# Row-tiled weighing in a two-layer graph network kernel: pairs of 64-row matmuls, bias by its own bf16 matmul, and a new split of the product sums

## The reference

```python
# layer 0: h has 64 values an edge, w has 4 paths of 8 x 8
h = jax.nn.relu(edge_feat @ W1 + b1)
w = (h @ W2 + b2).reshape(e, 4, MUL, MUL)
m0 = ALPHA * (einsum('ei,eio->eo', s_e * sh0, w_000) + C110 * einsum('eim,em,eio->eo', v_e, sh1, w_110))
m1 = ALPHA * (einsum('ei,em,eio->eom', s_e, sh1, w_011) + einsum('eim,eio->eom', v_e * sh0, w_101))
out0 = segment_sum(m0, dst); out1 = segment_sum(m1, dst)
# layer 1: the same with 64 hidden values from one distance an edge, weights R, spherical harmonics Y of the
# edge's direction, and an einsum over paths
R = jax.nn.relu(abs_distances[:, None] @ w1 + b1) @ w2 + b2
x = _layernorm(x + layer(x))   # after each layer
```

## Time and profile before

| | |
|---|---|
| median of 3 runs | 4531.57 us (4531.0 to 4543.85) |
| profiled execution | 4544.37 us, span 4542.6 us |
| mean granted TensorE clock | 0.922 of full speed |
| busy: PE, PEld, DVE, ACT, POOL | 83%, 49%, 87%, 52%, 70% |

### The profile page before, as it was taken

How to read it: one execution, slowest core, us unless ns; L and a number is a source line. 1 busy time by engine, 2 the same in 40 slices (tenths; PEclk the granted TensorE clock), 3 DMA queues, 4 the chain that set the end, 5 groups by cost and what they waited for, 6 DMA issues and landing times.

```text
span 4542.6 us, 66084 instructions
## 1 busy us (share of the span) xinstructions
PE 3766.9 (83%) x19258; PEld 2237.4 (49%) x19258; DVE 3963.2 (87%) x4658; ACT 2346.9 (52%) x6473; POOL 3167.3 (70%) x3145
## 2 busy tenths in 40 slices
PE   5887887888787878887189999999999999999995
PEld 3555555555555555555034444444444444444442
DVE  6878788787887788877889999999999999999998
ACT  2555555555555555555045555555555555555553
POOL 6777777777777777777266667766766777667661
PEclk7998898888888988888589999999999999999997
DMA  2111111111111111111322121212121212121221
GB/s 91 28 23 28 28 23 28 28 23 28 27 25 28 23 28 28 23 28 23 76 49 43 34 43 34 43 34 44 34 43 34 43 34 43 34 43 37 40 40 21
DMA packets 206517, 159.45 MB, mean 35 GB/s; under 512 B 123073, under 2 KB 186562, under 8 KB 199234
## 3 DMA queue, kind: packets, MB, share of 16 engines
q1 hardware_dynamic: 76978, 89.79, 8.4%
q0 software_dynamic: 100352, 51.58, 7.9%
q10 hardware_dynamic: 29170, 17.88, 1.4%
HBM read 148.58 MB, written 10.43 MB: 35 GB/s over the span
## 4 chain that ended last, share of the span: by engine, by line
POOL 35%; PE 31%; issue 22%; DVE 10%; DVEq 1%; POOLq 0%; DMA 0%; ACT 0%; SPq 0%; ACTq 0%
POOL rows L340 35%; PE wps L624 16%; PE red L637 15%; DVE prod L913 6%; DVE t_b L1086 1%; DVE sums L924 0%; DVE q L983 0%; DVE t_b L842 0%; DVE work L823 0%; DVEq L897 0%; POOLq L357 0%; DVEq L1151 0%; DVE work L1195 0%; DVE table L1193 0%; DVE node_a L1196 0%
## 5 line engine op out<-in xcount | busy, mean ns | idle before, releaser
L624 PE MATMUL wps<-w_sb,hidden 128*128 128x256 f32 (+1 forms) x6272 | 2185.5, 506 | 669.6 <-DVE prod L906 394.8
L340 POOL DMA_INDIRECT rows<-x_rows,src x1568 | 1544.1, 985 | 755.7 <-issue 468.5
L624 PEld LDWEIGHTS wps<-w_sb,hidden 128*128 128x128 f32 x6272 | 1305.1, 213 | 1489.4 <-issue 518.5
L340 POOL DMA_INDIRECT rows<-in_x,src x1568 | 1615.2, 1030 | 506.3 <-issue 499.4
L637 PE MATMUL red<-prod,ident 128*128 128x384 f32 (+1 forms) x3136 | 1200.5, 536 | 0.0
L924 DVE TENSOR_REDUCE sums<-prod 128x192 f32<-128x1536 f32 (+2 forms) x392 | 1099.2, 2823 | 0.0
L460 ACT ACTIVATE gap<-iota,slot_plan 128x128 bf16<-128x128 f32 x3136 | 956.6, 387 | 264.1 <-DVE t_b L1086 179.4
L913 DVE TENSOR_TENSOR prod<-wps,q 128x896 f32<-128x896 f32 x784 | 844.8, 1086 | 96.3 <-PE wps L624 95.4
L637 PEld LDWEIGHTS red<-prod,ident 128*128 128x128 f32 x3136 | 594.8, 190 | 584.3 <-issue 396.5
L488 ACT ACTIVATE split<-acc,slot_plan 128x32 f32<-128x32 f32 x1568 | 300.1, 302 | 664.6 <-PE acc L651 635.2
L899 DVE TENSOR_TENSOR prod<-wps,q 128x768 f32<-128x768 f32 x392 | 374.0, 954 | 126.6 <-PE wps L624 126.2
(11 more groups left out here) (112 smaller groups left out, 2372.6 us busy)
## 6 DMA issues: line engine op xcount, KB each, us to landing
mlp<-in_dist SPq DMA_DIRECT2D x98, 512.0 KB, 5.0
mlp<-in_feat SPq DMA_DIRECT2D x98, 256.0 KB, 2.9
rows<-in_x,src POOLq DMA_INDIRECT x1568, 2.4
rows<-x_rows,src POOLq DMA_INDIRECT x1568
frames<-prod ACTq DMA_DIRECT2D x4, 1764.0 KB, 5.9
geo<-frames ACTq DMA_DIRECT2D x98, 72.0 KB, 1.9
src<-in_src SPq DMA_DIRECT2D x196, 8.0 KB, 1.6
geo<-in_sh ACTq DMA_DIRECT2D x98, 32.0 KB, 1.8
```

The source lines that it names most:

```text
L340: nc.gpsimd.indirect_dma_start(out=rows[z][:, t, :], out_offset=None, in_=table_rows, in_offset=bass.IndirectOffsetOnAxis(ap=src_sb[z][:, ...
L624: ins = nc.tensor.matmul(wps[:, col:col + W_PATHS[n] * MM], hidden[:, z, e0:e0 + P], w2, start=True, stop=True)
```

## The change

The hidden layer of two neighbouring tiles now lies on the two halves of the partitions: tile 0 on partitions 0 to 63, tile 1 on 64 to 127, in half the columns. Weights are held twice, on both halves. A stage of `weigh` first writes the bias into both banks of its half of `wps` by two bf16 matmuls (a matrix of ones on 64 rows with the bias, cut in three bf16 parts on three rows), and then runs for each pair of tiles one matmul on the lower and one on the upper 64 rows, into different banks, accumulating. The host reorders the edge inputs to match; distances come in two DMAs instead of one, and the fill of `hidden` with zeros and ones goes.

PE sums 12 tiles in both layers instead of 8 and 9, in two banks of `red` with a copy each; DVE sums the last 4 in one reduction. For these 4 tiles the weight columns are in the order (path, o, i) and the products are written with i innermost, so that the reduction reads neighbours. `sums` has two slots, `acc` one. The orders of PE, ACT and DVE change as the diff shows. Some DVE operations are added before the loops (`split_bias`, twice).

```diff
-PE_TILES = ((0, 8), (0, 9))
-PE_HALVES = tuple(-(-PE_TILES[n][1] // HALF_TILES[n]) for n in range(2))
-DVE_SUMS = (((8, 12), (12, 16)), ((9, 12), (12, 16)))
+PE_SUMS = (((0, 8), (8, 12)), ((0, 6), (6, 12)))
+PE_TILES = 12
+DVE_TILES = TILES - PE_TILES
+BANKS = 2
...
-            nc.gpsimd.memset(hidden[HID:P, :, :], 0.0).then_inc(hidden_filled, 1)
-            nc.gpsimd.memset(hidden[HID:HID + 1, :, :], 1.0).then_inc(hidden_filled, 1)
...
             def hide(n, z, r, half):
 
                 s = layers[n]
-                c0 = half * 2 * SET
                 if half == 0:
                     act.wait_ge(s.weights_ready[z], r * HALVES[n])
                 if n == 0:
                     act.wait_ge(s.hidden_summed[z], r * 2 + half + 1)
-                    nc.scalar.activation(hidden[0:HID, z, c0:c0 + SET], hps[0:HID, :], ACT.Relu,
-                                         bias=b1_sb[0:HID, 0:1])
-                    nc.scalar.activation(hidden[0:HID, z, c0 + SET:c0 + 2 * SET], hps[HID:P, :], ACT.Relu,
-                                         bias=b1_sb[HID:P, 0:1]).then_inc(s.hidden_ready[z], 1)
+                    nc.scalar.activation(hidden[:, z, half * SET:(half + 1) * SET], hps[:], ACT.Relu,
+                                         bias=b1_sb[:, 0:1]).then_inc(s.hidden_ready[z], 1)
                 else:
                     if half == 0:
-                        act.wait_ge(s.mlp_loaded[z], r * 16 + 16)
-                    nc.scalar.activation(hidden[0:HID, z, c0:c0 + 2 * SET], mlp_sb[z][0:HID, c0:c0 + 2 * SET],
-                                         ACT.Relu, bias=b1_sb[0:HID, 1:2], scale=w1c_sb[:, 0:1]
-                                         ).then_inc(s.hidden_ready[z], 1)
+                        act.wait_ge(s.mlp_loaded[z], r * 32 + 32)
+                    nc.scalar.activation(hidden[:, z, half * SET:(half + 1) * SET],
+                                         mlp_sb[z][:, half * SET:(half + 1) * SET], ACT.Relu,
+                                         bias=b1_sb[:, 1:2], scale=w1c_sb[:, 0:1]).then_inc(s.hidden_ready[z], 1)
...
-            def copy_sums(n, z, r):
-
-                s = layers[n]
-                a, b = PE_TILES[n]
+            def copy_sums(n, z, r, bank):
+
+                s = layers[n]
+                a, b = PE_SUMS[n][bank]
                 cols = (b - a) * PATHS[n] * MUL
-                act.wait_ge(s.products_summed[z], r + 1)
-                nc.scalar.activation(sums_by_half(n)[:, :, a:b, :],
-                                     red[:, 0:cols].rearrange("p (h t c) -> p h t c", h=2 - n, t=b - a), ACT.Copy
-                                     ).then_inc(s.sums_copied[z], 1)
+                act.wait_ge(s.products_summed[z], r * BANKS + bank + 1)
+                nc.scalar.activation(sums_by_half(n, z)[:, :, a:b, :],
+                                     red[:, bank * 512:bank * 512 + cols].rearrange("p (h t c) -> p h t c", h=2 - n, t=b - a),
+                                     ACT.Copy).then_inc(s.sums_copied[z], 1)
...
                         distances(n, z1, r1, 1, steps)
-                        if n == 0:
+                    if n == 0:
+                        if not tail:
                             one_hots(n, z1, steps)
-                    if not last:
-                        hide(n, z, r + 1, 0)
-                        if n == 1:
+                            copy_sums(n, z1, r1, 0)
+                            copy_sums(n, z1, r1, 1)
+                        if not last:
+                            hide(n, z, r + 1, 0)
                             hide(n, z, r + 1, 1)
-                    if n == 1:
+                        split_windows(n, z, r)
+                    else:
+                        if not last:
+                            hide(n, z, r + 1, 0)
+                            hide(n, z, r + 1, 1)
                         if not tail:
+                            copy_sums(n, z1, r1, 0)
                             one_hots(n, z1, steps)
                         if not last:
                             copy_rows(n, i + 1, z, r + 1)
-                    if n == 0:
-                        split_windows(n, z, r)
+                        if not tail:
+                            copy_sums(n, z1, r1, 1)
                         if not last:
-                            hide(n, z, r + 1, 1)
-                    if n == 1 and not last:
-                        complete_q(z, r + 1)
-                    if not tail:
-                        copy_sums(n, z1, r1)
-                    if n == 1:
+                            complete_q(z, r + 1)
                         split_windows(n, z, r)
...
-                    for t in range(T):
-                        col = (q % 2) * 1024 + t * (1024 // T)
-                        e0 = (q * T + t) * P
-                        ins = nc.tensor.matmul(wps[:, col:col + W_PATHS[n] * MM], hidden[:, z, e0:e0 + P], w2,
-                                               start=True, stop=True)
+                    oi = int(summed_by_dve(n, q))
+                    w2 = w2_oi[n][:] if oi else w2_sb[n][:, 0].rearrange("p a c -> p (a c)")
+                    C, B = W_PATHS[n] * MM, T // 2
+                    base = (q % 2) * 1024
+                    for a in range(2):
+                        nc.tensor.matmul(wps[:, base + a * 512:base + a * 512 + B * C], ones[a * HID:(a + 1) * HID, :],
+                                         bias_parts[n][a * HID:(a + 1) * HID, oi:oi + 1, :].broadcast_to([HID, B, C]),
+                                         start=True, stop=False)
+                    for b in range(B):
+                        e0 = (q * B + b) * P
+                        for a in range(2):
+                            col = base + a * 512 + b * C
+                            ins = nc.tensor.matmul(wps[:, col:col + C], hidden[a * HID:(a + 1) * HID, z, e0:e0 + P],
+                                                   w2[a * HID:(a + 1) * HID, :], start=False, stop=(b == B - 1))
                     ins.then_inc(s.weights_ready[z], 1)
...
-            def sum_products(n, z, r):
-
-                s = layers[n]
-                a, b = PE_TILES[n]
+            def sum_products(n, z, r, bank):
+
+                s = layers[n]
+                a, b = PE_SUMS[n][bank]
                 cols = (b - a) * PATHS[n] * MUL
                 pr = products(n)
-                pe.wait_ge(s.weights_used[z], r * HALVES[n] + PE_HALVES[n])
-                pe.wait_ge(s.sums_copied[1 - z], r + z)
+                pe.wait_ge(s.weights_used[z], r * HALVES[n] + -(-b // HALF_TILES[n]))
+                pe.wait_ge(s.sums_copied[1 - z], (r + z) * BANKS - (BANKS - 1 - bank))
                 for i in range(MUL):
-                    ins = nc.tensor.matmul(red[:, 0:cols], ident[:], pr[:, i, :, a:b, :], start=(i == 0),
-                                           stop=(i == MUL - 1))
+                    ins = nc.tensor.matmul(red[:, bank * 512:bank * 512 + cols], ident[:], pr[:, i, :, a:b, :],
+                                           start=(i == 0), stop=(i == MUL - 1))
                 ins.then_inc(s.products_summed[z], 1)
...
-                pe.wait_ge(s.windows_split[z], r)
+                pe.wait_ge(s.windows_split[1 - z], r + z)
...
                     if n == 0:
                         weigh(n, z1, r1, range(2, H))
+                        sum_products(n, z1, r1, 0)
+                        sum_products(n, z1, r1, 1)
                         if not last:
                             sum_hidden(n, z, r + 1, 0)
                         scatter(n, z, r)
                         if not last:
                             sum_hidden(n, z, r + 1, 1)
-                        sum_products(n, z1, r1)
-                        if not last:
                             weigh(n, z, r + 1, (0, 1))
                     else:
-                        weigh(n, z1, r1, range(2, H - 2))
-                        sum_products(n, z1, r1)
-                        weigh(n, z1, r1, range(H - 2, H))
+                        weigh(n, z1, r1, range(2, 5))
+                        sum_products(n, z1, r1, 0)
+                        weigh(n, z1, r1, range(5, H))
+                        sum_products(n, z1, r1, 1)
                         if not last:
                             weigh(n, z, r + 1, (0, 1))
                         scatter(n, z, r)
...
-            def sum_tiles(n, z, r, which, st):
+            def sum_tiles(n, z, r, st):
+
+                s = layers[n]
+                dve.wait_ge(s.weights_used[z], r * HALVES[n] + HALVES[n])
+                st.done(nc.vector.tensor_reduce(sums_by_half(n, z)[:, :, PE_TILES:TILES, :], products_oi(n), AX_X, ALU.add))
```

234 lines of the change are left out of this document (126 added, 108 removed).

## The result

| | before | after |
|---|---|---|
| median of 4 runs | 4532.6 us (4531.0 to 4543.85) | 4377.66 us (4374.53 to 4378.6) |
| profiled execution | 4544.37 us, span 4542.6 | 4377.07 us, span 4375.3 |
| ratio of the medians | | 0.9653, 95% interval 0.9639 to 0.9668 |

The change makes the kernel 3.5% faster. The forecast was 4380 us, so the total is right within 3 us.

A forecast was written before the change was run, and what follows sets the result against it. The prediction took POOL's gathers to bound layer 0, and PE and DVE compute layer 1. Gains of 117 (layer 1), 29 (layer 0) and 6 us (ends) make 152; 4531.6 - 152 = 4380 us, range 4310 to 4530.

The forecast's parts named there:

- A gain of 0.3 us x 98 = 29 us: Layer 0: gathers meet shorter runs of DVE additions with two SBUF operands, saving 0.3 us in each of 98 chunks.
- the excess of 1.1 us a chunk: Layer 0: gather time above the undisturbed 0.94 us each, 1.4 us a chunk before, taken as 1.1 after (0.9 to 1.6).
- PE's stage of weighing: Layer 1, PE: bias and four fp32 records, stages 1.34 us apart with ordered weight loads; 0.95 full overlap, 1.89 serial.
- rival (a): Layer 1: the row halves overlap freely, PE needs 19.4 us, POOL binds at 20.8; gain 201 us, 4331 us; chance 0.17.
- (c): Weighing on PE: the halves do not overlap, a stage takes 1.89 us, PE 25.7 us a chunk; 4811 us; chance 0.17.
- rival (b): PE: changing between 64-row and 128-row matmuls empties the array, six changes cost 1.0 us a chunk; 4467 us; chance 0.18.
- the forecast 21.3: Layer 1: PE sets the chunk at 21.3 us, from 22.49 before, a gain of 117 us over 98 chunks.
- POOL (20.6 to 21.1) right behind: Layer 1: POOL's gathers need 20.6 to 21.1 us a chunk, just under PE's 21.3, so POOL is not the bound.
- the prediction's own signs: Layer 1, if right: PE at 97% or more, weighing stages 1.3 us apart; POOL in the chain would mean wrong.
- Ends: Last chunk's chain, layer 1's prologue and layer 0's last body: shorter sums save about 2 us each, 6 in all.
- At most -1: Setup: the memsets POOL loses (2 x 3.5 us) end 1.4 us after DVE's part is ready; effect at most -1.
- DVE's terms: Layer 1: reductions fall from 5.72 to 2.01 us, multiplications stay 1086 ns, DVE's busy time from 21.6 to 17.9 us a chunk.

The follow-up runs named there:

- before_parted_half: Kernel before; layer 0: DVE operations in the changed kernel's order; layer 1: 8 instead of 16 gathers a chunk. 4437.56 us, ratio to before 0.9786.
- clustered_half: Changed kernel; layer 0: additions to windows 0 and 1 moved between L1063 and L1067; layer 1: 8 of 16 gathers a chunk. 4252.61 us, ratio to before 0.9378.
- split2_b: Changed kernel; layer 1's frame multiplication (L1121) and projection (L994) each cut in three, other operations between the thirds, order otherwise kept. 4310.39 us, ratio to before 0.9507.
- before_parted: Kernel before with only layer 0's DVE operations in the changed kernel's order, on the chip where before takes 6812.7 us. 6933.85 us, ratio to before 1.0187.
- the free rearrangement: Changed kernel; layer 1's frame multiplication and projection cut in thirds, the eight multiplications put between, nearly every operation moved. 4501.05 us, ratio to before 0.993.

## Why the prediction was right, and where it was not

**The bounds of before: right.** Layer 0 was POOL's, layer 1 was compute's. before_parted_half confirms both: an edit that shortens gathers is worth 100 us in layer 0, and halving the gathers changes layer 1's chunk by 0.02 us.

**Layer 0: right mechanism, size a third of what it was.** "A gain of 0.3 us x 98 = 29 us (bounds: gain 50, loss 16)" was 102. The step that failed is the excess of 1.1 us a chunk and its lower end of 0.9: it became 0.36. The prediction treated gathers as if they met DVE's operations at random, in shorter runs than before. They meet them at fixed phases. The excess sat in three gathers of the chunk (medians 1.22, 1.64 and 1.25 us in the 2nd, 4th and 7th), and the new order removed two of them outright: only the 2nd is left, 1.21 us, beside the projection that starts when rows land. In the changed kernel, timeline of layer 0:

```profile
1016.22 0.56 DVE L990 TENSOR_TENSOR t_a<-rows,geo 128x384 f32<-128x384 f32 x1 [6.79 <-DMA rows<-in_x,src]
1016.31 1.28 POOL L350 DMA_INDIRECT rows<-in_x,src  x1 [0.30 <-issue]
```

DVE's wait for rows grew from the 289 us of the earlier trace rows to 677, as said.

**DVE: right.** The remaining reductions and the multiplications, by form:

```profile
L968 DVE TENSOR_REDUCE sums<-prod 128x224 f32<-128x1792 f32 x98 | 197.0, 2010 | 0.1
L968 DVE TENSOR_REDUCE sums<-prod 128x192 f32<-128x1536 f32 x98 | 170.7, 1741 | 0.0
L959 DVE TENSOR_TENSOR prod<-wps,q 128x896 f32<-128x896 f32 x784 | 834.8, 1082 | 198.9 <-PE wps L642 175.7 <-DVE sums L968 22.0 <-DVE q L1025 0.2
```

2.01 and 1.74 us were forecast for the reductions, from two rows of other sizes, and 1086 ns for the multiplications.

**PE's stage of weighing: the mis-sized term.** It was priced at 1.34 us by a load row, between 0.95 and 1.89. The trace shows 0.95. Changed kernel, PE at 3006 to 3013 (start, length of the group; x2 and x4 are both halves together):

```profile
3006.42 0.92 PE L642 MATMUL wps<-w_sb,hidden 64*128 64x448 f32 x4
3007.27 4.79 PE L655 MATMUL red<-prod,ident 128*128 128x336 f32 x16
...
3011.99 0.36 PE L635 MATMUL wps<-bias_parts,ones 64*128 64x448 bf16 x2
3011.99 0.39 PEld L642 LDWEIGHTS wps<-w_sb,hidden 64*128 64x128 f32 x4
3012.19 0.92 PE L642 MATMUL wps<-w_sb,hidden 64*128 64x448 f32 x4
...
3012.94 0.35 PE L635 MATMUL wps<-bias_parts,ones 64*128 64x448 bf16 x2
```

From 3011.99 to 3012.94 is one stage: 0.20 for both bias matmuls together and 0.75 for four fp32 records in two steps of 0.372. The records of the two halves start 3 to 4 ns apart. The loads, four in 0.39 us, do not hold them in order; that was the assumption behind 1.34. This is the full overlap, the prediction's lower end and shorter than the 1.12 that rival (a) used, and no sign of (c).

**The emptying of the array, rival (b): real, but smaller.** Four records take 0.75 us where weighing follows (3012.19 to 3012.94) and 0.85 where sums follow (3006.42 to 3007.27). Record by record, from start to start, it is 466 instead of 372 ns into the sums, and 378 instead of 282 out of them; from one stage of 64 rows into the next it stays at 372. That makes 0.095 us a change, not 0.16, and 0.6 us in a chunk of layer 1. The Trainium skill (TensorEngine Tiling (Array Packing), Tiling Modes, Key Properties) says that a change of mode drains the engine; the trace agrees. Together PE needs 8 x 0.95 + 9.0 + 1.4 + 0.6 = 18.6 us, and the chain of compute 19.6 by clustered_half, against the forecast 21.3.

**Layer 1: PE was to set 21.3 us, and POOL set 22.2.** "POOL (20.6 to 21.1) right behind" was the step that failed: it took the gather mean of 985 ns from a trace in which POOL was not the bound. The change moved DVE's order, and the bound itself moved the phases, since DVE now starts L994 on the landing of rows (read from the timeline above; neither was undone alone). The mean rose to 1067, and cutting the two operations in split2_b brought it back to 1022. The gain came to 28.8 + 25.2 = 54 us instead of 117. Rival (a), which names the right mechanism, gave 166 for this layer by the same mistake. By the prediction's own signs this layer was wrong: PE is busy 88% and not 97% or more, stages are 0.95 us and not 1.3, and POOL is in the chain.

**Ends.** The prologue and the head gave 6.9 + 4.5 us where 6 were forecast in all. "At most -1" for the fills is too little by the rows above: DVE's part was ready at 15.84 and the fills ended at 17.24, but the all-reduce began only at 26.09, after an issue gap of 8.84 us that is gone in the changed kernel. The traces of before_parted and before_parted_half, which keep the fills, have the gap too (7.6 and 7.9 us); split2_b and clustered_half, without them, begin the all-reduce at 16.8 and 16.6. The fills were not taken out alone, so that they cause the gap is likely and not shown. The first gather came 6.9 us sooner.

**Sum.** +73 in layer 0, -63 in layer 1 and +5 at the ends make +15 against the forecast gain of 152. The profiled execution of before was 12 us above its median, so the medians differ by 155. The point was right by luck. Both large errors are about the length of a gather, too long in the forecast of layer 0 and too short in that of layer 1, and they had opposite signs. What was sound is the bound of each layer before, DVE's terms, and the sign and rough size of the whole.

## What to carry to other kernels

When POOL issues indirect DMAs on the critical path, read each gather's length by its place in the loop, not as a mean, and look which DVE operation with two SBUF operands runs beside the long ones; cutting or moving these operations pays (100 us by order alone in layer 0, 67 us by cutting two operations in layer 1). A pace read off an engine that is not the bound is no forecast of its pace when it becomes the bound. In an order written by hand even a small move can lengthen a chain of waits, so read the chain after each: the free rearrangement lost 123 us, two moved additions lost 0.9 us a chunk (clustered_half), and the cut that kept the order won 67.

## What the hardware showed that was not expected

- Two fp32 matmuls of 64 rows on the two row halves, into different banks, run at the same time: starts 3 to 4 ns apart, four records of 448 columns in 0.75 us, a whole stage with bias in 0.95.
- A change between 64-row and 128-row matmuls costs 0.095 us (466 instead of 372 ns, 378 instead of 282).
- A gather that starts during a DVE operation with two SBUF operands ends 0.82 us after that operation, whatever is left of it: 0.82 us behind one of 1.35 us, 0.81 behind one of 0.55. The Trainium skill (SBUF — State Buffer, SBUF: two separate sides) describes this lock, with an end about 115 ns after the DVE operation, measured with a DMA that takes about 620 ns alone, beside a copy. Here it is 0.82 us. That is near the gather's whole undisturbed 0.94, so the work of the gather seems to start only after the operation.
- Gathers that begin with such an operation escape. In the kernel before, 204 gathers of layer 1 started in L1086 or L952, or up to 0.1 us before, with over 0.15 us to go; 116 of them ended before the operation did. The border is sharp: in both kernels those that start up to 0.03 us after the operation's start take their 0.94 us, and from 0.05 us on each of them ends 0.82 us after it.
- The same kernel before takes 4532 to 4536 us beside most runs and 6812 us on one other chip, and the edit of DVE's order in layer 0 wins 100 us in the one case and loses 125 in the other.
